# A two-network graph kernel: all eight heads of a graph turned in 32x32 blocks on VectorE and moved from SBUF to SBUF, and the first network's exponentials taken ahead of the transposes on ScalarE

## The reference

```python
# first network: 3 layers, one attention head
for l in range(3):
    scores = si[:, :, None] + sj[:, None, :] + attn_b[l]          # si, sj = x @ attn_w[l, :d], x @ attn_w[l, d:]
    scores = jnp.where(scores >= 0, scores, 0.2 * scores)
    attn = softmax(jnp.where(mask, scores, -inf), axis=-1)        # mask: adjacency or diagonal
    h = layernorm(x + attn @ x, g1[l], beta1[l])                  # 512 x 512 times 512 x 256
    ff = gelu(h @ W1[l] + b1[l]) @ W2[l] + b2[l]                  # 256 -> 1024 -> 256
    x = layernorm(h + ff, g2[l], beta2[l])
# then x = layernorm(x_in + x)
# second network: 8 heads of width 32
scores = leaky_relu(a_src[:, :, :, None] + a_dst[:, :, None, :] + b_att, 0.2)
att = softmax(jnp.where(A > 0, scores, NEG_INF), axis=-1)          # per head 512 x 512
out = relu(einsum('bhij,bhjk->bhik', att, xh))                     # then layernorm(x + out)
```

## Time and profile before

| | us or share |
|---|---|
| median of 3 runs (lowest to highest) | 2327.34 (2326.52 to 2328.55) |
| the profiled execution's own time, and its span | 2329.5, 2327.7 |
| TensorE busy, instructions | 2187.7 us, 94%, 10117 |
| VectorE busy, instructions | 1863.9 us, 80%, 5743 |
| ScalarE busy, instructions | 1636.4 us, 70%, 3151 |
| GpSimd busy | 201.8 us, 9% |
| DMA | 315.74 MB, 162145 packets |
| mean granted TensorE clock | 0.984 |

### The profile page before, as it was taken

One profiled execution on the slowest core, in us unless ns is written; L12 is line 12 of the kernel. 1 busy time (PEld: TensorE's weight loads), 2 busy tenths in 40 slices (PEclk: granted clock), 3 DMA queues, 4 the chain that ended last, 5 costly groups with the idle time before them and its releaser, 6 DMA issues.

```text
span 2327.7 us, 31621 instructions
## 1 busy us (share of the span) xinstructions
PE 2187.7 (94%) x10117; PEld 1525.1 (66%) x10117; DVE 1863.9 (80%) x5743; ACT 1636.4 (70%) x3151; POOL 201.8 (9%) x200
## 2 busy tenths in 40 slices
PE   5999998999999999999999999999999999999766
PEld 3766666676667667667766766676676667667453
DVE  5566587688888888888888888888888888877867
ACT  2344467777787777778777777777777777778676
POOL 0000100010101001010100101010010101001000
PEclk9999999999999999999999999999999999999888
DMA  6011133227455362735436274553627455364201
GB/s 219 1 36 55 47 108 127 86 87 236 131 179 157 114 213 86 245 122 186 150 123 206 85 241 125 178 158 114 212 86 229 138 171 165 97 202 153 92 28 37
DMA packets 162145, 315.74 MB, mean 136 GB/s; under 512 B 10392, under 2 KB 82620, under 8 KB 153532
## 3 DMA queue, kind: packets, MB, share of 16 engines
q1 hardware_dynamic: 161980, 313.72, 42.5%
HBM read 235.82 MB, written 77.86 MB: 135 GB/s over the span
## 4 chain that ended last, share of the span: by engine, by line
PE 71%; DVE 20%; ACT 5%; issue 2%; POOL 1%; DMA 1%; DVEq 0%; SPq 0%; POOLq 0%; ACTq 0%
PE ffn L1341 19%; PE av L1258 14%; PE av L1330 10%; PE ffn L1330 10%; PE pT L1240 7%; PE av L1282 4%; DVE prob L846 3%; DVE prob L837 2%; DVE stats L778 2%; PE av L1317 1%; DVE lone L806 1%; PE av L1365 1%; PE trow L1365 1%; DVE xs L972 1%; DVE xs L966 1%
## 5 line engine op out<-in xcount | busy, mean ns | idle before, releaser
L1341 PE MATMUL ffn<-w_sb,G 128*128 128x256 f32 x3072 | 724.1, 381 | 12.5 <-ACT G L560 12.5
L1341 PEld LDWEIGHTS ffn<-w_sb,G 128*128 128x128 f32 x3072 | 571.1, 191 | 94.1 <-ACT G L560 18.1
L846 DVE CUSTOM_DVE_ANT_0 prob<-trow,mask 128x512 f32<-128x512 f32 x676 | 438.5, 686 | 31.7 <-PE trow L1219 19.6
L1330 PE MATMUL ffn<-hT,w_sb 128*128 128x512 f32 x768 | 364.0, 601 | 4.4 <-DVE xs L959 1.3
L1330 PE MATMUL av<-hT,w_sb 128*128 128x512 f32 x768 | 358.2, 596 | 0.0
L500 POOL TENSOR_TENSOR rstd<-veps,mhalf 128x4 f32<-128x4 f32 x127 | 170.5, 1342 | 2087.4 <-DVE veps L774 2087.4
L536 ACT ACTIVATE prob<-prob,s 128x512 f32<-128x512 f32 x484 | 329.4, 715 | 7.7 <-DVE aw_row L853 4.3
L542 ACT ACTIVATE prob<-prob,nm 128x512 f32<-128x512 f32 x464 | 329.2, 714 | 0.0
L1240 PEld LDWEIGHTS pT<-ident,prob 128*128 128x128 f32 x1648 | 208.2, 144 | 134.0 <-issue 103.3
L1240 PE MATMUL pT<-ident,prob 128*128 128x128 f32 x1648 | 251.3, 278 | 27.2 <-DVE prob L908 14.6
L1330 PEld LDWEIGHTS ffn<-hT,w_sb 128*128 128x128 f32 x768 | 140.1, 191 | 152.2 <-issue 134.1
(11 more groups left out here) (164 smaller groups left out, 2739.5 us busy)
## 6 DMA issues: line engine op xcount, KB each, us to landing
w_sb<-in_L_gnn_W SPq DMA_DIRECT2D x92, 1024.0 KB, 8.8
blocks_dram<-blocks SPq DMA_DIRECT2D x264, 256.0 KB, 4.2
prob<-blocks_dram SPq DMA_DIRECT2D x66, 1024.0 KB, 4.9
trow<-rows_dram SPq DMA_DIRECT2D x127, 256.0 KB, 3.7
adj_sb<-in_adj SPq DMA_DIRECT2D x16, 1024.0 KB, 9.0
xin<-in_x SPq DMA_DIRECT2D x16, 512.0 KB, 6.0
x0r<-in_x SPq DMA_DIRECT2D x16, 512.0 KB, 10.0
out<-o SPq DMA_DIRECT2D x15, 512.0 KB, 6.9
```

What stands on the lines that cost most here:

```text
L846: return v.tensor_tensor_reduce(out=out_[:, t, :], in0=targets, in1=mask[:, t, :], scale=1.0, scalar=LEAST, op0=ALU.add, op1=ALU.max, accu ...
L1330: last = te.matmul(ff1[f % len(ff1)][:], w1_sb[:, weights_of(g) % STAGES, dt, f * P:(f + 1) * P], hT[:, dt, :], start=dt == 0, stop=dt == ...
L1341: last = te.matmul(ffn[part][:, at:at + D], G[:, f, t * P:(t + 1) * P], w2_sb[:, weights_of(g) % STAGES, f, :], start=f == 0, stop=f == FT ...
```

## The change

1. BY_BLOCKS becomes all eight heads: 104 heads are turned by VectorE where 66 were. turned_ahead is the first moved head of every unit, turned_behind all others; in g % 3 == 0 the first head is turned ahead, the second behind the attention and the third at the unit's end.
2. move issues 16 transfers (32 partitions x 512) straight from blocks to ring(q); blocks_dram is gone. VectorE's next turn waits until all 16 have landed (s_moved).
3. The first network's exponential is taken on ScalarE with nm0 as its bias, ahead of the transposes (first_exponential); first_exponents on VectorE is gone, and probabilities copies. All four tiles are done before any head's work on ScalarE (first_network_probabilities).
4. The output's last scaling (graph_out) goes to ScalarE in all but the last graphs (normalise(LAST, ...), ahead of targets_out in g % 3 == 1); GpSimd makes its shift.
5. find_lone moves from g % 3 == 0 to g % 3 == 2, behind keep_masks; of make_masks the first half (mask_edges) moves ahead of the attention in g % 3 == 0, the second (mask_diagonal) stays.
6. TensorE has one more piece ahead of the attention, one fewer behind it; the four heads' product in g % 3 == 0 stands behind f == 4, not 3.

The diff, cut to its core:

```diff
-BY_BLOCKS = (1, 2, 4, 6, 7)
+BY_BLOCKS = tuple(range(HEADS))
...
 def turned_ahead(g):
-    return [q for q in turned(g) if moved(q)][:1] if g % 3 != 1 else []
+    return [q for q in turned(g) if moved(q)][:1] if g > min(FIRST_MADE) + 1 else []
 def turned_behind(g):
-    if g % 3 == 1:
-        return [q for q in turned(g - 1) + turned(g) if moved(q)][-2:] if g > 1 else []
-    return [q for q in turned(g) if moved(q)][1:] if g % 3 == 2 else []
+    return [q for q in turned(g) if moved(q)][len(turned_ahead(g)):]
 def spent_behind(g):
-    return 3 if g % 3 == 0 else 1
+    return 4 if g % 3 == 0 and HEADS - 3 in BY_BLOCKS else 1
+def masked(g):
+    return g // 3 + 1 if g > 3 and g % 3 == 0 and g // 3 + 1 < GRAPHS else None
...
             def move(q):
                 n = moves(q) - 1
-                i = n % BANKS
                 sp.wait_ge(s_block, n + 1)
-                if n >= BANKS:
-                    sp.wait_ge(s_moved, 16 * (n - BANKS + 1))
-                for a in range(BLOCKS):
-                    sp.dma_start(blocks_dram[i, :, :, a, :].rearrange("b j n -> j b n"),
-                                 blocks[a * BLOCK:(a + 1) * BLOCK, :, :]).then_inc(s_left, 16)
-                sp.wait_ge(s_left, 16 * BLOCKS * (n + 1))
-                sp.dma_start(ring(q)[:], blocks_dram[i].rearrange("b j a n -> (b j) a n")).then_inc(s_moved, 16)
+                for b in range(BLOCKS):
+                    for a in range(BLOCKS):
+                        sp.dma_start(ring(q)[b * BLOCK:(b + 1) * BLOCK, a, :],
+                                     blocks[a * BLOCK:(a + 1) * BLOCK, b, :]).then_inc(s_moved, 16)
...
+            def first_exponential(t):
+                act.wait_ge(s_score0, c("score0"))
+                nc.scalar.activation(prob0[:, t, :], prob0[:, t, :], ACT.Exp, bias=nm0[:, t:t + 1], scale=1.0).then_inc(s_arg, 1)
             def probabilities(t):
                 act.wait_ge(s_pt, c("pt"))
-                nc.scalar.activation(prob0[:, t, :], pT[t % BANKS][:], ACT.Exp).then_inc(s_prob, 1)
+                nc.scalar.copy(prob0[:, t, :], pT[t % BANKS][:]).then_inc(s_prob, 1)
+            def first_network_probabilities(u, scored):
+                first_exponential(0)
+                for t in range(1, T):
+                    if t >= scored:
+                        score0(u, t)
+                    first_exponential(t)
+                    probabilities(t - 1)
+                probabilities(T - 1)
...
+                if leaving(g) is not None:
+                    normalise(LAST, o1, o1, s_out)
...
                 if n:
-                    dve.wait_ge(s_left, 16 * BLOCKS * n)
+                    dve.wait_ge(s_moved, 16 * BLOCKS * BLOCKS * n)
...
                 for q in turned_ahead(g):
                     turn_blocks(q)
+                if masked(g) is not None:
+                    mask_edges(masked(g) % 2)
                 attention(graph2, l2, *new[1:2])
...
                 elif g > 3 and g % 3 == 2:
                     keep_masks(g // 3 % 2)
-                elif g > 3 and g % 3 == 0 and g // 3 + 1 < GRAPHS:
-                    find_lone((g // 3 + 1) % 2)
-                    make_masks((g // 3 + 1) % 2)
+                    if g // 3 + 2 < GRAPHS:
+                        find_lone(g // 3 % 2)
+                elif masked(g) is not None:
+                    mask_diagonal(masked(g) % 2)
...
-                ahead, inside, behind = (4, (1, 1), (1, 1, 1, 1)) if four is None else (2, (2, 1), (2, 1, 2, 1))
+                ahead, inside, behind = (5, (1, 1), (1, 1, 1, 0)) if four is None else (3, (2, 1), (2, 1, 1, 1))
```

More of the change, by code:

```diff
@@ L52 @@
 OWN_PLACE = (LAST_HEADS - SIDE, LAST_HEADS - SIDE + 1)
-ATTENDED, RESIDUAL, FED, LAST = range(4)
+ATTENDED, RESIDUAL, LAST, FED = range(4)
 COLS = LAYERS * (2 * DT + FT)
@@ L283, in build @@
         s_score0, s_arg, s_score1, s_exp = sem("score0"), sem("arg"), sem("score1"), sem("exp")
-        s_block, s_left, s_moved = sem("block"), sem("left"), sem("moved")
+        s_block, s_moved = sem("block"), sem("moved")
         s_pt, s_prob, s_pd, s_copy = sem("pt"), sem("prob"), sem("pd"), sem("copy")
@@ L289, in build @@
         s_av1, s_oT, s_back, s_av1e = sem("av1"), sem("oT"), sem("back"), sem("av1e")
-        s_ve, s_rstd, s_shift = sem("ve"), sem("rstd"), [sem("shift0"), sem("shift1")]
+        s_ve, s_rstd, s_shift = sem("ve"), sem("rstd"), [sem(f"shift{i}") for i in range(3)]
         s_hn, s_hT, s_hTe, s_ff1, s_gelu = sem("hn"), sem("hT"), sem("hTe"), sem("ff1"), sem("gelu")
@@ L601, in _ @@
                 score0(0, t)
-            for t in range(T):
-                probabilities(t)
+            first_network_probabilities(0, T)
             act.wait_ge(s_colT, 1)
@@ L678, in _ @@
                 gelu(1, f)
-                if f >= T:
+                if f >= T and not moved(first - 2):
                     turned_out(first - 2, f - T)
@@ L702, in _ @@
                 score0(UNITS - 2, t)
-            for t in range(T):
-                probabilities(t)
+            first_network_probabilities(UNITS - 2, T)
             for t in range(T):
@@ L771, in aggregate @@
                 dve.wait_ge(s_dch, c("dch"))
-                if which in (ATTENDED, RESIDUAL):
-                    v.tensor_scalar(nmean[which][:], mv[:, :, 0], -1.0, None, ALU.mult)
+                if which != FED:
+                    v.tensor_scalar(nmean[which][:], mean[:, :, 0], -1.0, None, ALU.mult)
                 v.tensor_scalar_add(veps[which][:], mean[:, :, 1], EPS).then_inc(s_ve, 1)
@@ L1071, in _ @@
             first_targets(0)
-            for t in range(T):
-                first_exponents(t)
             dve.wait_ge(s_const, 16 * CONSTS)
@@ L1147, in _ @@
             plus_bias(GRAPHS - 1, 1)
-            turn_blocks(first - 3)
+            for q in turned_ahead(REGULAR):
+                turn_blocks(q)
             head_made(second)
             fed_forward(GRAPHS - 1, 0)
-            turn_blocks(first - 1)
+            for q in turned_behind(REGULAR):
+                turn_blocks(q)
             head_made(third)
@@ L1268, in attend_heads @@
             def attend_heads(q):
-                by_act, by_vector = all_out[[h for h in range(q, q + SIDE) if not moved(h)][-1], T - 1]
-                pe.wait_ge(s_prob, by_act)
-                if by_vector:
-                    pe.wait_ge(s_copy, by_vector)
+                by_engine = [h for h in range(q, q + SIDE) if not moved(h)]
+                if by_engine:
+                    by_act, by_vector = all_out[by_engine[-1], T - 1]
+                    pe.wait_ge(s_prob, by_act)
+                    if by_vector:
+                        pe.wait_ge(s_copy, by_vector)
                 if any(moved(q + i) for i in range(SIDE)):
-                    pe.wait_ge(s_moved, 16 * moves(q + SIDE - 1))
+                    pe.wait_ge(s_moved, 16 * BLOCKS * BLOCKS * moves(q + SIDE - 1))
                 pe.wait_ge(s_x1Te, turning[0])
@@ L1417, in _ @@
                         for q in heads[:1]:
-                            turn(q, f - T)
+                            if not moved(q):
+                                turn(q, f - T)
                 pieces(ahead)
```

47 lines of the change are left out of this document (23 added, 24 removed).

## The result

The changed kernel takes **2624.7 us** (median of 4 runs, 2622.2 to 2632.0) against 2328.0 us of the kernel before beside it (2326.5 to 2328.6): ratio 1.128, 95% interval [1.126, 1.131]. Forecast were 2421 us, 2359 to 2480. The sign was right and the loss three times too small: +297 us for +94. Nearest came the rival with the slow moves (2600 us, chance 0.08).

A forecast was written before the change was run, and what follows sets the result against it. TensorE was taken to be full for 106 of each three-unit period's 135 us, VectorE holding the rest; 0.4 + 7.0 - 0.4 + 1.05 = +8.1 us a period, together +94, gave 2421 us, range 2359 to 2480.

The forecast's parts named there:

- the rival with the slow moves: Rival, chance 0.08: a move takes 13.5 us, both waits and the rows' store grow, +24.5 us a period, 2600 us.
- The moves: Each turned head's 16 SBUF-to-SBUF transfers: 5.4 us of issues plus 2.4 for the last landing, 7.8 us a move.
- E2 to E0: Last attention product of g % 3 == 2 to that of g % 3 == 0: +7.0 us, 50.75 for 43.77.
- E0 to N1: Last attention product of g % 3 == 0 to ScalarE's two Prelus of g % 3 == 1: -0.4 us before move waits.
- N1 to E2: ScalarE's two Prelus of g % 3 == 1 to the last attention product of g % 3 == 2: +0.4 us.
- Who waits: Waits for moves in g % 3 == 0: TensorE 3.7 us before the four heads' product, VectorE 1.05 us.
- TensorE's two stalls: In g % 3 == 0, before the fourth first-network product 4.9 us, before the four heads' product 3.7 us.
- VectorE's third turn in slot 0: In g % 3 == 0, this turn waits for the second's move to free blocks: +1.05 us a period.
- Nothing queued behind the moves on SyncE is urgent: SyncE's queue: the next weights, held behind the moves, are wanted over 40 us later; no cost.
- The hidden case: Rival, chance 0.2: a move under 5.4 us causes no waits; +4.9 us a period, 2386 us.
- The first seven units ... 0: Start of the run: no moved heads and the same TensorE work, so 0 us change.
- The clock: Rival, chance 0.15: TensorE's granted clock falls at the new 4.9 us stall; 2.6 us a period, 2450 us.

The follow-up runs named there:

- e2: The changed kernel with only 1 of each move's 16 transfers issued, the other blocks left unmoved: 2388.8 us.
- e3: The changed kernel with all 16 transfers a move, each of half its columns and so half its bytes: 2620.6 us.
- e11: The changed kernel with four transfers a move, each 256 KB over all 128 partitions, in place of 16: 2392.2 us.
- e1: The changed kernel with only 9 of each move's 16 transfers issued, the other blocks left unmoved: 2418.7 us.
- e7: The changed kernel with one transfer a move, the first head of g % 3 == 2 turned by TensorE again: 2383.9 us.
- e15: The changed kernel with one transfer a move, the first network's exponentials back on VectorE: 2399.4 us.
- e6: The kernel before with only the first network's exponentials moved to ScalarE: 2395.2 us.
- e10: The changed kernel with moves by way of DRAM, the first leg cut into 16 transfers of 64 KB: 2582.4 us.
- e8: The changed kernel with each move's 16 transfers split, eight issued by SyncE and eight by GpSimd: 2510.5 us.
- e14: The kernel before with the mask's first half and find_lone moved ahead of the attention of g % 3 == 0: 2389.2 us.
- e13: The kernel before with only the mask's first half moved ahead of the attention of g % 3 == 0: 2333.2 us.

## Why the prediction was wrong

**The step that failed** is *The moves*, the issue time of one transfer: "16 x 0.34 = 5.4", from "a quarter of the bytes should stay near the first, or near the 0.34". An issue took 0.63 us from start to start, and a move 11.5 us where the sum had 7.8; "a move longer than 10 us" was the prediction's own sign of being wrong. Both rows it leaned on were of other kinds: one issue alone, and transfers with DRAM at one end. From SBUF to SBUF an issue costs 0.51 us even alone (e2), 0.59 in a row, at half the bytes (e3) as at four times the bytes (0.61, e11). That bytes make the old leg's later issues longer was right of that leg (0.43 us at 64 KB, up to 1.24 at 256 KB), and did not carry over. The upper bound, 16 x 0.68 from the same group, came nearer, 13.5 us for 11.5, but by luck: its mean of 0.68 holds one issue of 1.24 us, and the change's own issues show no such growth (0.59 from the second to the last, medians).

The term carried the sum: at 7.1 us (e1) the kernel takes 2418.7 us, at 11.5 us 2624.7. That is 47 us of run time for each us of move between the two, 3.9 a period. SyncE issues moves for 1664 x 0.63 = 1050 us in all and holds the chain for 22% of 2630, 579 us: over half of the issue time is on the chain, since blocks is one buffer and the rows' store is in the same queue. By stretches, for 4.4 us of move more: E2 to E0 grows by 7.9 (by the rows shown, the longer move 4.4, the wait for blocks in slot 2 0.9, the clock behind the second stall 2.2), E0 to N1 by 4.5 (the third turn), N1 to E2 by 3.8 (the target rows, for which VectorE waits).

**Who waits** was right for three of the waits: TensorE's two stalls (5.30 and 4.64 for 4.9 and 3.7 us), VectorE's third turn in slot 0. That last wait is seen in few periods of e1 (six waits for blocks in the whole run, 0.77 to 5.36 us), where the forecast had 1.05 in each. The waits for blocks in slots 2 and 1 it did not have, and "Nothing queued behind the moves on SyncE is urgent" held at 7.1 us (15.7 us of waits for the rows in all, before 28.4) and not at 11.5 (73.6); only the slow rival had a price for it. e7 shows one turn's share of the first stall, 2.21 of 4.33 us; that the other 2.12 are find_lone's is the prediction's sum, and no run took find_lone out.

**The hidden case** was priced at 2386 us and measured at 2388.8. Two errors cancel in it. "The first seven units ... 0" was wrong: even with free moves the change is 10.5 us behind by unit 7 and 15.6 by unit 10, where the sum had some 2 (ahead of the attentions of units 2 and 3 TensorE waits 2.30 us for a normalised state where it waited 1.43; for the rest, e15 puts some 6 us by unit 10 down to the exponentials, and some stays open). Against that, a period lost 4.6 to 5.0 us in the first half, as forecast (4.9), but 3.0 to 4.0 in the second, where the kernel before is slower itself. That e1 comes out at 2418.7 for 2421 is the same luck: at its 7.1 us the prediction's own sum, with both waits 0.7 us shorter, gives 2406 us.

**N1 to E2, +0.4**: nearly right (62.4 us with short moves, before 62.5 and later more), but as a difference of larger parts. The exponentials alone cost 1.2 to 1.5 us a slot (e6); a head's turn given back to TensorE costs 1.8 us in slot 2 (e7), so the turns taken off it pay them back.

**E0 to N1, -0.4**: right with short moves (28.5 us in e2 for 29.0).

**The clock** was a rival, and is part of the slow case. In e1 its loss behind the first stall passes under the wait for the move; in the change so do 2.6 us of it, and 2.2 us a period behind the second stall do not.

**The slow moves**, 2600 us, came nearest, and in part by chance. Its three prices were for a move of 13.5 us; at 11.5 two of them shrink by 2 us each. What it lacked, the clock and the wait in slot 2, filled the gap: 22.5 us a period for its 24.5. The 25 us it is short of the time are the start (some 14 us beyond the sum's part) and what comes behind unit 43, where the change loses 34 us for a forecast of about 3, less some 17 us that the full periods stay under the price. Its chance of 0.08 was too low beside 0.44 for the forecast: both lengths came from one group of rows, and none of them was SBUF to SBUF.

## What to carry to other kernels

Count transfers before bytes: a queue that issues short transfers in a row pays for each, here 0.63 us, and everything behind it in that queue pays too. A price read from one kind of transfer (into DRAM, out of DRAM, alone) need not hold for another: measure the kind that the change uses. Where a kernel is tightly interlocked, a latency is not paid once: ask how many of its copies lie on the chain before trusting a value between two bounds, and let the chances follow the bounds. And parts of such a change don't add: moving the exponentials lost 67 us in the old order and won 11 in the new, measured with one transfer a move.

## What the runs showed of the hardware

Issue on SyncE, by form: DRAM to SBUF 0.34 us for 1 MB; SBUF to DRAM 0.32 alone, 0.43 in a row at 64 KB (e10), and 0.33, 0.43, 0.59 and 1.24 for four of 256 KB in a row (before); SBUF to SBUF 0.51 alone, 0.59 in a row for 32 and 64 KB into 32 partitions, 0.47 and 0.61 for 256 KB over 128. On GpSimd's queue 0.50 (e8). Landing 2.0 us for 64 KB into 32 partitions (the change), 2.4 for 256 KB over 128 (e11); on GpSimd's queue 32 of 808 took over 4 us. The granted clock was 1.00 in the 12 us up to 1241, and 0.64 over the 12 us from 1245, which hold the end of the stall of 5.30 us, the products behind it and the stall of 4.64. Products ran slow behind stalls of 4.3 us and more (the change, e1, e2, e14) and at full rate behind those of 2.12 (e7) and 1.57 us (e13).
